# An attention kernel's work order rewritten: block transposes between the two heads' mask steps, output transposes a pair later, moves issued from two queues

## The reference, cut to what matters

```python
q = (M @ Wq.T).reshape(e, h, dh).transpose(1, 0, 2)
k, v = jnp.split(x @ Wkv.T + bkv, 2, axis=-1)
sim = jnp.einsum('hid,hjd->hij', q, k) * dh ** (-0.5)
sim = jnp.where(mask, sim, -1000000000.0)
attn = jax.nn.softmax(sim, axis=-1)
out = jnp.einsum('hij,hjd->hid', attn, v).transpose(1, 0, 2).reshape(e, h * dh)
m = layer_norm(out @ Wo.T + bo + M)
z = layer_norm(jax.nn.relu(m @ W1.T + b1) @ W2.T + b2 + m)
```

## Time and profile before

| | us |
|---|---|
| median of three runs | 787.69 |
| the profiled execution | 788.94 |
| its span | 787.1 |
| PE busy | 674.7 (86%) |
| DVE busy | 581.0 (74%) |
| ACT busy | 367.6 (47%) |
| POOL busy | 163.0 (21%) |

### The profile page before, as it was taken

How to read it: one execution, slowest core, us unless ns; L and a number is a source line. 1 busy time by engine, 2 the same in 40 slices (tenths; PEclk the granted TensorE clock), 3 DMA queues, 4 the chain that set the end, 5 groups by cost and what they waited for, 6 DMA issues and landing times.

```text
span 787.1 us, 10971 instructions
## 1 busy us (share of the span) xinstructions
PE 674.7 (86%) x3382; PEld 404.6 (51%) x3382; DVE 581.0 (74%) x715; ACT 367.6 (47%) x658; POOL 163.0 (21%) x239
## 2 busy tenths in 40 slices
PE   4888888899888888898898888888898849699995
PEld 3664444544445444554455444554455425478884
DVE  4498898778887799779987898879878771633333
ACT  4355455554545455555554554555544530333332
POOL 2200320023100420023100320033000070421213
PEclk8889999999999999999999999999999969799998
DMA  8067788767787678868787678867777884022321
GB/s 304 1 155 171 161 181 210 190 157 167 174 237 177 146 179 212 198 140 180 175 237 178 154 175 221 195 142 179 168 170 175 267 192 106 28 80 82 105 80 53
DMA packets 52503, 127.95 MB, mean 163 GB/s; under 512 B 15744, under 2 KB 16256, under 8 KB 52224
## 3 DMA queue, kind: packets, MB, share of 16 engines
q1 hardware_dynamic: 52480, 127.67, 66.5%
HBM read 23.80 MB, written 1.05 MB: 32 GB/s over the span
## 4 chain that ended last, share of the span: by engine, by line
PE 64%; SPq 14%; DVE 10%; issue 6%; DMA 3%; ACT 2%; POOL 0%; DVEq 0%; ACTq 0%; POOLq 0%
PE tail L834 18%; PE slot L807 16%; SPq L366 13%; PE tail L736 10%; PE slot L736 7%; PE slot L887 6%; PE slot L895 5%; DVE st L665 3%; DVE prob L652 3%; DMA pt<-st 2%; DVE k_lo L604 1%; DMA wq_raw<-in_wq 1%; PE tail L841 1%; ACT val L539 1%; DVE stats L689 1%
## 5 line engine op out<-in xcount | busy, mean ns | idle before, releaser
L533 ACT ACTIVATE prob<-prob,negmax 128x896 f32<-128x896 f32 x224 | 234.1, 1045 | 274.7 <-DVE negmax L652 274.7
L652 DVE CUSTOM_DVE_ANT_0 prob<-slot,lower,negmax_old 128x896 f32<-128x896 f32 x224 | 248.8, 1148 | 77.5 <-PE slot L807 73.9
L665 DVE STREAM_TRANSPOSE st<-prob 128x1792 f32<-128x1792 f32 x112 | 228.6, 2041 | 19.8 <-DMA pt<-st 19.3
L834 PE MATMUL tail<-pt,val 128*64 128x512 f32 x784 | 209.4, 664 | 0.4 <-DMA pt<-st 0.4
L807 PE MATMUL slot<-k_hi,q_hi 64*128 64x448 f32 x448 | 98.1, 432 | 50.4 <-DVE k_lo L604 39.5
L834 PEld LDWEIGHTS tail<-pt,val 128*64 128x64 f32 x784 | 54.2, 152 | 110.6 <-issue 110.6
L807 PEld LDWEIGHTS slot<-k_hi,q_hi 64*128 64x128 f32 x448 | 44.0, 191 | 106.1 <-issue 63.4
L807 PE MATMUL slot<-k_hi,q_lo 64*128 64x448 f32 x448 | 88.2, 386 | 0.0
L807 PE MATMUL slot<-k_lo,q_hi 64*128 64x448 f32 x448 | 87.3, 382 | 0.0
L441 POOL TENSOR_TENSOR total<-total,alpha 128x8 f32<-128x8 f32 x28 | 5.8, 206 | 249.8 <-ACT alpha L554 249.8
L807 PEld LDWEIGHTS slot<-k_hi,q_lo 64*128 64x128 f32 x448 | 45.9, 198 | 3.5
(11 more groups left out here) (107 smaller groups left out, 844.1 us busy)
## 6 DMA issues: line engine op xcount, KB each, us to landing
pt<-st SPq DMA_DIRECT2D x896, 112.0 KB, 2.3
w_raw<-in_w SPq DMA_DIRECT2D x32, 256.0 KB, 2.8
x_raw<-in_x SPq DMA_DIRECT2D x6, 896.0 KB, 5.8
mask_raw<-in_mask SPq DMA_DIRECT2D x7, 448.0 KB, 3.9
mt_raw<-in_mt SPq DMA_DIRECT2D x2, 512.0 KB, 8.0
wq_raw<-in_wq SPq DMA_DIRECT2D x2, 512.0 KB, 8.7
wo_raw<-in_wo SPq DMA_DIRECT2D x1, 1024.0 KB, 4.7
m_res<-in_mn SPq DMA_DIRECT2D x1, 1024.0 KB, 6.9
```

What stands on the lines that cost most here:

```text
L533: nc.scalar.activation(unit, unit, ACT.Exp, bias=negmax[:, p, u:u + 1], scale=-1.0, accum_out=psumrow[:, p, u:u + 1]).then_inc(exp_done, 1)
L652: nc.vector.tensor_tensor_reduce(out=prob[:, i % 2, h].rearrange("p (b n) -> p b n", b=2), in0=slot[:, j, :, :HALF], in1=lower[:, i].rearr ...
L665: nc.vector.transpose(st[:, g].rearrange("p b k (t i) -> p k b t i", t=2)[:, :, :, t2], prob[:, i % 2].rearrange("p h (k b i) -> p (h k) b ...
L834: last = nc.tensor.matmul(outT[DH * h:DH * h + DH], val[:, i, head(p, h)], moving, start=(i == 0), stop=(i == KT - 1))
```

## The change

The list is now read from a table of words, `ROUNDS`, one string for each round of each pair. For pair 2 it is

```diff
-                        for turn in range(QUAD):
+                        for turn in (0, 1, 2):
@@
-                    if kind == "B":
+                    if kind == "T":
                         act.wait_ge(aoT_filled, p + 1)
...
+                    if kind == "B":
+                        buf = move_buf(p, i)
...
+                        act.wait_ge(xposed, written)
+                        for turn in (3,):
+                            for a in (0, 2, 1, 3):
+                                b = (a + turn) % QUAD
+                                act.dma_start(pt[LANES * b:LANES * b + LANES, buf, a],
+                                              st[LANES * a:LANES * a + LANES, i, b]).then_inc(landed[buf], 16)
@@
-                    if kind == "S":
+                    if kind in "SU":
...
-                        for h in range(2):
+                        for h in ((0,) if kind == "S" else (1,)):
@@
-            def tp_free(c, kind, p, i):
...
+            def bank_plan(sched):
+
+                plan, last = {}, None
+                for step in sched:
+                    if step[0] in "VF":
+                        plan[step], last = last, step
+                return plan
+
+            def tp_free(c, before):
+
+                if before is None and isinstance(c, int) and c == 0:
+                    pe.wait_ge(qlo_done, PAIRS)
+                elif before is None:
+                    pe.wait_ge(acc_added, pair_no(c, -PAIRS) + 1)
+                elif before[0] == "V":
+                    pe.wait_ge(v_copied, KT * c + before[2] + 1)
                 else:
-                    pe.wait_ge(acc_added, pair_no(c, p))
+                    pe.wait_ge(acc_added, pair_no(c, before[1]) + 1)
```

More of the change, by code:

```diff
@@ L41 @@
 PAIR_LANDED = 16 * QUAD * QUAD
+ROUNDS = (
[16 rows of a table added]
+)
 def chunk_schedule(first, last):
     out = []
[L53 to L59, removed]
-    for p in range(PAIRS):
[L62 to L137, removed]
@@ new lines, in chunk_schedule @@
+    for p in range(PAIRS):
+        for t in range(QT):
+            for word in ROUNDS[p][t].split():
+                kind, i = word[0], int(word[1:] or 0)
+                step = (kind, p, i)
+                if kind in "SU":
+                    step = (kind, p, t)
+                elif kind == "E":
+                    step = (kind, p, (t, i))
+                elif kind == "X":
+                    step = (kind, p, t - 1) if t else (kind, p - 1, QT - 1)
+                elif kind == "V":
+                    step = (kind, 0, i)
+                elif kind in "WC":
+                    step = (kind, p - 2, i)
+                elif kind in "FA":
+                    step = (kind, p - 3, i)
+                elif kind in "KHL":
+                    step = (kind, p + 1, i)
+                elif kind in "MB":
+                    step = (kind, p - i, i)
+                elif kind == "Z":
+                    step = (kind, p - 1, i)
+                if first and step[1] < 0 or last and (kind in "JRQ" or step[1] == PAIRS) or not last and kind in "IO":
+                    continue
+                out.append(step)
+                if kind == "A" and last and step[1] >= 0:
+                    out.append(("N", step[1], 0))
@@ L138, in chunk_schedule @@
     if last:
         a, b = PAIRS - 2, PAIRS - 1
[L140 to L144, removed]
@@ L145, in chunk_schedule @@
-        out.extend([("Y", 1, 1), ("Y", 1, 2), ("Y", 1, 3), ("G", b, 0), ("B", b, 0), ("D", b, 0)])
+        out.extend([("F", 1, 0), ("A", 1, 0), ("N", 1, 0)])
+        out.extend([("X", b, 3), ("M", b, 1), ("B", b, 1), ("Z", b, 0)])
+        out.extend([("G", 0, 0), ("T", 0, 0), ("D", 0, 0)])
+        out.extend([*(("W", a, kt) for kt in range(3)), ("G", 1, 0), ("T", 1, 0), ("D", 1, 0)])
+        out.extend([*(("W", a, kt) for kt in range(3, KT)), ("C", a, 0), ("Y", 0, 0), ("F", a, 0), ("A", a, 0), ("N", a, 0)])
@@ L146, in chunk_schedule @@
+        out.extend([("Y", 0, 1), ("Y", 0, 2), ("Y", 0, 3), ("G", a, 0), ("T", a, 0), ("D", a, 0)])
+        out.extend([*(("W", b, kt) for kt in range(KT)), ("C", b, 0), ("Y", 1, 0), ("F", b, 0), ("A", b, 0), ("N", b, 0)])
+        out.extend([("Y", 1, 1), ("Y", 1, 2), ("Y", 1, 3), ("G", b, 0), ("T", b, 0), ("D", b, 0)])
         out.extend([("Y", 2, t) for t in range(QT)])
@@ L633, in body @@
                     n = pair_no(c, p)
[L634 removed]
+                    if kind in "SU":
                         masks = taken = None
[L636 removed]
+                        if kind == "S" and p == 0 and (i == 0 or not final):
                             masks = in_register(dve, CHUNKS * QT + 1 if final else c * QT + i + 1)
[L638 removed]
+                        if kind == "S" and i == 0 and is_past(n, PAIRS):
                             taken = in_register(dve, 2 * (n - PAIRS + 1))
                         free = in_register(dve, QT * n + i - 1) if is_past(QT * n + i, 2) else None
[L641 removed]
+                        for h in ((0,) if kind == "S" else (1,)):
                             j, before = unit_use(c, p, i, h)
@@ L772, in project @@
                 return last
-            def tp_free(c, kind, p, i):
[L776 to L789, removed]
+            def bank_plan(sched):
[11 more added lines that the diff above has]
+                    pe.wait_ge(v_copied, KT * c + before[2] + 1)
                 else:
-                    pe.wait_ge(acc_added, pair_no(c, p))
+                    pe.wait_ge(acc_added, pair_no(c, before[1]) + 1)
             def body(c, sched):
-                for kind, p, i in sched:
+                banks = bank_plan(sched)
+                for step in sched:
+                    kind, p, i = step
                     n = pair_no(c, p)
@@ L811, in body @@
                     if kind == "V":
-                        tp_free(c, kind, p, i)
+                        tp_free(c, banks[step])
                         products(tp, lambda a, k: x2[a][:, k, P * i:P * i + P], lambda m, k: wv2[m][:, k],
@@ L845, in body @@
                         if p == 0:
[L846 to L850, removed]
+                            emptied = dict(unit_use(c, PAIRS - 1, t, h) for t in range(QT) for h in range(2))
+                            for j in range(RING):
+                                pe.wait_ge(drained[j], emptied[j] + 1)
                         if p >= 2:
```

9 lines of the change are left out of this document (7 added, 2 removed), and 16 rows, old and new, of the table ROUNDS.

## The result

The changed kernel takes 895.6 us (median of 4, 892.56 to 896.6) against 787.37 us before (four runs of each): the ratio is 1.1365, 95% interval 1.1338 to 1.1392. The forecast was slower, 862 us with a range up to 892. The direction was right, the size was not: +108 us instead of +74, and outside the range. The profiled execution has a span of 893.4 us, 106.3 more than before. One execution further down, of the experiment f_late, ran in a slower state (879.7 us, at a lower granted clock than the other three) and is left out of its times.

What follows compares the result with a forecast made beforehand. Neither PE nor DVE alone bounds; the hand-overs within a round set the time. Five chunks at +12.1, +8 for the first chunk and +5.5 at the end make +74 us on 788.9, less 1.25: 862 us, range 816 to 892.

Steps and rivals of the forecast that it cites:

- The S behind L, uncovered in round 3: Round 3, every pair: nothing on DVE covers PE's S (1.43 us); 6.85 us, against 5.74 (pairs 2, 3), 7.51 (pair 1).
- V5 behind A: Pair 2's round 1: V5 waits for A, behind both mask steps and X; 8.85 us against 4.87, the largest term, +4.0.
- Round 0 and the clock: Round 0: W at low clock in pairs 0, 3; 5.85 us there and in pair 2, 6.9 in pair 1.
- Round 2: Round 2: S waits for the second mask step behind X; 5.8 us against 4.94 in pairs 0, 3; 6.7 elsewhere.
- The ends: First chunk +8 us (two thirds of a chunk's loss), last chunk and what follows it +5.5 us.
- Two queues: SP issues 12 of 16 DMAs, ACT 4 at 0.63 us each; saves only issue time, costs nothing on ACT.
- SP's queue is the real bound: Rival, chance 0.07, 766 us: relieving SP's queue gives back all 19.3 us, DVE's new order costs nothing.
- X's wait for exponentials: X waiting for ACT's exponentials: 0.2 to 0.3 us a round where DVE runs free, hidden by the wait for PE.
- The milder rival: Rival, chance 0.17, 837 us: low clock falls into longer idle stretches instead of over W in round 0, 25 us less.
- dear issues: Rival, chance 0.12, 900 us: ACT's issues cost about 2 us each, hold up exponentials, X waits (+28), V5's clock +10.

Runs made afterwards that it cites:

- f_late: The changed kernel with F and A of pair 2 moved from round 1 to round 3; 870.5 us, ratio 1.105.
- l_early: The changed kernel with round 3 alone put back to S, U, L, X in all four pairs; 837.1 us, ratio 1.065.
- filled: The changed kernel with unused matmuls in PE's idle stretch of round 3 in pairs 0, 2 and 3; 866.6 us, ratio 1.0985.
- before_filled: The kernel before, all moves on SP, with unused matmuls ahead of PE's wait for L; 782.2 us, ratio 0.9941.
- split_filled: The kernel before with its moves on two queues and unused matmuls ahead of PE's wait for L; 758.4 us, ratio 0.964.
- late_filled: The changed kernel with pair 2's F and A in round 3 and unused matmuls filling PE in round 3; 843.9 us, ratio 1.071.

## Why the prediction was wrong in size

The step that failed is the price of PE's work behind the two new waits. The sum took it at the full clock: 1.43 us for the S behind L, 2.50 for V5 and W4 behind A. The runs show the lower clock there: 2.54 and 4.13.

- **The S behind L, uncovered in round 3.** Right in place and mechanism (l_early: 59 us), but mis-sized. The sum took 6.85 us; measured are 8.05, 8.06 and 8.67 in pairs 2, 3 and 0, of which S's 2.54 explains 1.1 each (filled shows it: with S at 1.43 the round is 6.95) and X's wait for moved blocks 0.5 in pair 0. I had read the low clock at one place, where only the W behind S carried it, and charged it to W alone. The other places in the same trace, with S at up to 2.31 us, were there to be read. I also read PE as idle from 371.94 to 375.5, but F lies in that stretch (371.86, 0.66 us long): the wait was 2.94 us. The new waits are 4.4 to 7.0 us.
- **V5 behind A.** Right that V5 waits, 3.4 us in the trace, 3.2 forecast. Mis-sized in the same way: 10.58 us instead of 8.85. I had named 1.7 us a chunk for the clock here and left it to the range's upper end; V5 and W4 took 1.6 us more, so it belonged in the sum. The Trainium skill's page "TensorE: Matmul & The Clock Gate", section "HAM oscillation — how this bites in real kernels", on which I had leaned for it, says that repeated idle gaps between groups of matmuls drop the clock each time. The trace agrees: 0.50 behind V5's gap.
- **Round 0 and the clock.** Forecast 6.9 in pair 1, measured 6.19; 5.85 in pairs 3 and 0, measured 5.91 (415.28 to the next round) and 5.53. The low clock did not move from W to S: behind pair 2 it lay on both, S 2.54 and W 4.5. In the chunk shown, rounds 3 of pairs 2, 3 and 0 are together 4.23 us above the forecast, V5's round 1.73, and all the other rounds together 1.26 below it: 4.70, the difference between 104.95 and 100.25.
- **Round 2.** Forecast 5.8, measured 5.95 in pair 0 (5.93 in pair 3). Pairs 1 and 2 as forecast, 6.43 and 6.72 against 6.7.
- **The ends.** I took +8 for the first chunk, measured +15.3: each of its four pairs grew by 3.5 to 4.5 us. In the steady chunks pair 1 loses next to nothing because its round 3 was 7.5 us already; in the first chunk that round took 6.1 us before and 8.2 after, and two thirds of a steady chunk's loss missed that. From the start of chunk 6 on I took +5.5, measured +10.5. The span's growth of 106.3 exceeds the sum's 74 by 32: 21.5 in the five chunks, 7.3 in the first, 5 behind them, less 1.5 at the start.
- **Two queues.** Right: no loss on ACT, issue time only. Its value depends on the rest: it gains 4.5 us alone, but 24 once PE's clock stays up (before_filled against split_filled). I counted only what SP's queue held up in the kernel before. The rival "SP's queue is the real bound" was wrong for this change and half right for the kernel.
- **X's wait for exponentials.** Right, 0.2 us in all.
- **The milder rival**, that the low clock would fall into the idle stretches, went the other way: behind the longer idle stretches the whole S runs at the low clock, and in part the W as well. The "dear issues" rival landed near the measured time for the wrong reason; 0.61 us an issue excludes it.
- One thing said of the change is not one: the x load stood behind that M in the list before, too. It entered no term.

What stays open: how much of the extra loss at the ends is the low clock and how much the order of the steps there; why S and W together lose 1.4 us to the low clock in one place (from 309.57 us) and 2.9 in another (from 412.50), behind the same wait of 4.4 us; and the low clock that late_filled keeps in pair 1.

## What to carry to other kernels

Before moving a step on the engine that hands work to PE, ask what lay over PE's answer. Here X covered the S that waits for `k_lo`, and when it moved away, PE's time and two hand-overs came onto the path, in round 3 of three pairs and in round 2 of two. The waits that newly stopped PE here, of 3.4 us and more, cost more than their length: where a trace shows the low clock behind a shorter wait, price the work behind a longer one at it, in the sum and not in the range. Read such a place more than once, since one of them may be the exception. And two bounds of nearly the same size hide each other, so try their cures together: fill and split gave 5 and 4.5 us apart, and 29 together.

## What was not expected of the hardware

- Useless work made the kernel faster. In the kernel before with two queues, 10 or 7 unused 128x512 matmuls ahead of PE's wait for L took 782.7 us to 758.4, at a mean granted clock of 1.00 instead of 0.95 in the loop (130 to 600 us). With all moves on SP the clock rose as much and the time fell by 5 us only.
- ACT's queue issues one of these DMAs (32 partitions, 112 KB) in 0.61 us, median, against SP's 0.59; from issue to landing they took 2.5 and 2.3 us. SP took 10.05 to 10.08 us for the 16 of one M, 0.63 each, and 0.67 each over 86 of them in a row.
